# Feed-forward of a four-layer image network: three PSUM banks in turn for the centred tiles, and the slots written out

## What is computed

```
t = t + ffn(layernorm(t))          # 24 -> 96 -> relu -> 24, products in an 8-bit float, sums rounded to fp16
x = x + next_mixer(layernorm(x))   # the mixer of the following layer begins with a norm over the channels
```

## Time and profile before

| | us |
|---|---|
| median of three runs (lowest, highest) | 3311.95 (3308.96, 3316.39) |
| the profiled execution's own time | 3312.04 |
| its span, from first to last instruction | 3310.4 |
| busy over the span: PE, DVE, ACT, POOL | 2831.6, 2666.6, 2258.8, 1860.7 |
| stretch 1, from first to last instruction | 462.6 to 629.3 |
| stretch 2 | 1971.3 to 2142.2 |
| stretch 3 | 2676.0 to 2847.2 |
| stretch 4 | 3165.3 to 3307.1 |

### The profile page before, as it was taken

How to read it: one execution, slowest core, us unless ns; L and a number is a source line. 1 busy time by engine, 2 the same in 40 slices (tenths; PEclk the granted TensorE clock), 3 DMA queues, 4 the chain that set the end, 5 groups by cost and what they waited for, 6 DMA issues and landing times. The chain is left out here.

```text
span 3310.4 us, 65685 instructions
## 1 busy us (share of the span) xinstructions
PE 2831.6 (86%) x20846; PEld 1477.4 (45%) x20846; DVE 2666.6 (81%) x4380; ACT 2258.8 (68%) x4205; POOL 1860.7 (56%) x1466
## 2 busy tenths in 40 slices
PE   8999989686999999999997678789999779688876
PEld 5666654233444444444442224344444334477732
DVE  6888879536999999999999958769999968444468
ACT  5666658576999898989895427666777558444455
POOL 2333323155889898989897635447777745100046
PEclk9999999898999999999999999989999989899999
DMA  2000001256474747474746232201101012301023
GB/s 88 0 0 0 0 14 45 81 172 175 120 209 135 221 140 222 140 217 141 217 124 185 59 79 74 76 21 25 24 23 25 18 56 89 126 22 23 22 71 78
DMA packets 201533, 294.28 MB, mean 89 GB/s; under 512 B 62242, under 2 KB 179158, under 8 KB 201110
## 3 DMA queue, kind: packets, MB, share of 16 engines
q1 hardware_dynamic: 198678, 288.03, 30.3%
q10 hardware_dynamic: 2688, 4.29, 0.4%
HBM read 190.11 MB, written 102.09 MB: 88 GB/s over the span
## 5 line engine op out<-in xcount | busy, mean ns | idle before, releaser
L1780 POOL TENSOR_TENSOR mam_hc<-mam_h,mam_cs 128x896 f32<-128x896 f32 x336 | 703.5, 2094 | 173.5 <-DVE mam_h L1699 98.7
L1699 DVE TENSOR_TENSOR_SCAN mam_h<-mam_a,mam_kept,mam_dbx 128x448 f32<-128x448 f32 x672 | 737.7, 1127 | 48.4 <-ACT mam_a L1569 47.4
L1422 PE MATMUL mam_ps_y<-mam_hc,mam_ident 128*128 128x448 f32 x1344 | 570.8, 558 | 124.8 <-POOL mam_hc L1780 124.7
L1569 ACT ACTIVATE mam_a<-mam_ft,mam_a_neg 128x448 f32<-128x448 f32 x672 | 409.5, 657 | 77.1 <-DVE mam_h L1699 76.0
L1422 PEld LDWEIGHTS mam_ps_y<-mam_hc,mam_ident 128*128 128x128 f32 x1344 | 249.8, 193 | 425.4 <-POOL mam_hc L1780 216.2
L1686 DVE TENSOR_TENSOR mam_dbx<-mam_ps_u,mam_bs 128x448 f32<-128x448 f32 x672 | 380.7, 610 | 0.0
L682 POOL TENSOR_TENSOR att_prob<-att_prob,att_share 128x588 f32<-128x588 f32 x128 | 149.0, 1186 | 306.8 <-DVE att_share L974 306.8
L2209 POOL TENSOR_TENSOR scan_ch<-scan_h,scan_cs 128x392 f32<-128x392 f32 x192 | 263.7, 1387 | 56.5 <-DVE scan_h L2150 55.3
L368 POOL MEMSET f_squares_ln<- 128x392 f32 x4 | 1.7, 424 | 362.5 <-POOLq L2283 326.5
L387 POOL CAST f_h<-f_hr 128x392 fp8e5<-128x392 f16 x128 | 65.3, 510 | 234.1 <-DVE f_hr L308 234.1
L2150 DVE TENSOR_TENSOR_SCAN scan_h<-scan_decay_by_column,scan_h,scan_drive_by_column 128x392 f32<-128x392 f32 x112 | 196.8, 1757 | 0.0
(11 more groups left out here) (240 smaller groups left out, 6631.1 us busy)
## 6 DMA issues: line engine op xcount, KB each, us to landing
mam_taps<-normed SPq DMA_DIRECT2D x220, 130.5 KB
mam_bs<-dram_bc SPq DMA_DIRECT2D x56, 448.0 KB, 9.1
mam_cs<-dram_bc SPq DMA_DIRECT2D x56, 448.0 KB, 11.7
normed<-f_staged SPq DMA_DIRECT2D x96, 203.0 KB
mam_ft<-dram_steps SPq DMA_DIRECT2D x42, 448.0 KB, 4.8
f_mixed<-mixed SPq DMA_DIRECT2D x64, 196.0 KB, 2.4
mam_gt<-dram_gs SPq DMA_DIRECT2D x48, 224.0 KB, 2.7
dram_gs<-mam_gs SPq DMA_DIRECT2D x47, 224.0 KB, 2.8
```

The costliest lines, as they stand in the source:

```text
L1422: mm = pe.matmul(ps_y[p % 2][:, 0:MT], ident[:], hc[t % 2][:, i, :], start=False, stop=(t % 8 == 7 and i == 1))
L1569: act.activation(a[t % 3][:, i, :], ft[p % 2][:, 0, :], ACT.Exp, scale=a_neg[:, at:at + 1]).then_inc(decays, 1)
L1699: dve.tensor_tensor_scan(h[:, n % 8, :], a[t % 3][:, i, :], dbx[:, i, 0:MT], kept[:, at:at + 1], ALU.mult, ALU.add).then_inc(scanned, 1)
L1780: pool.tensor_tensor(hc[t % 2][:], h[:, row:row + 2, :], cs[:, 2 * pair:2 * pair + 2, :], ALU.mult).then_inc(weighed, 1)
```

## The change

The two banks of the feed-forward norm and the one of the mixer's norm become a ring of three. Centred tiles are written in one fixed order (norm of chunk s-3, then feed-forward of chunk s+1), and each takes the next bank of the ring. So the mixer's centred tile no longer waits for the tile of its own kind before it; the feed-forward tile that follows now waits for that (`normed` of chunk c-5 is behind `c - 4` in the code). All slots are written out on PE, ACT and DVE, with constant wait values. On POOL the loop is written with another index.

```diff
-        fronts = [buf.psum(f"xc_ff{p}", [P, BANK]) for p in range(2)]
-        xc_ln = buf.psum("xc_ln", [P, BANK])
+        ring = [buf.psum(f"centred{p}", [P, BANK]) for p in range(3)]
...
-            with eng.Fori(0, CHUNKS // UNROLL - 1) as t:
-                for i in range(3, 3 + UNROLL):
-                    slot(t * UNROLL + i, t + i // UNROLL, i % UNROLL, [True] * 4)
...
+        end = CHUNKS + (2 if last else lag)
+
+        def bank(c):
+            return ring[2 * c % 3]
+
+        def second_bank(c):
+            return ring[(2 * c + 1) % 3]
...
-                quantize_third(0)
-                for c in range(CHUNKS):
-                    if c + 1 < CHUNKS:
-                        quantize_third(c + 1)
-                    update(c)
+                for c in range(CHUNKS + 1):
+                    if is_chunk(c):
+                        quantize_third(c)
+                    if is_chunk(c - 1):
+                        update(c - 1)
                     if c + AHEAD_ADDED < CHUNKS and not in_place:
                         add_mixed(c + AHEAD_ADDED)
...
+                def subtract_mean(c):
+
+                    if not in_place:
+                        pe.wait_ge(ff["added"], c + 1 + ab)
+                    reached(pe, ff["quantized"], c - 2 + fb)
+                    if not last:
+                        reached(pe, ln["normed"], c - 4 + nb)
+                    centre_of(ff, bank(c), c)
+
+                def subtract_mean_again(c):
+
+                    pe.wait_ge(ff["updated"], c + 1 + fb)
+                    pe.wait_ge(ff["quantized"], min(c + 3, CHUNKS) + fb)
+                    reached(pe, ln["normed"], c - 2 + nb)
+                    centre_of(ln, second_bank(c), c)
...
-                slots(pe, slot)
+                for s in range(end):
+                    if is_chunk(s - 1):
+                        hidden_units(s - 1)
+                    if is_chunk(s - 2):
+                        second_product(s - 2)
+                    if not last and is_chunk(s - lag):
+                        subtract_mean_again(s - lag)
+                    if is_chunk(s + 1):
+                        subtract_mean(s + 1)
+                    if not last and is_chunk(s - lag):
+
+                        pe.wait_ge(ff["summed16"], min(s - 1, CHUNKS) + fb)
+                        variance(ln, "ln", nb, s - lag)
+                    if is_chunk(s + 1):
+                        variance(ff, "ff", fb, s + 1)
```

More of the change, by code:

```diff
@@ L188, in feed_forward_phase, with is_chunk @@
         lag = 3
[L190 to L195, removed]
-            with eng.Fori(0, CHUNKS // UNROLL - 1) as t:
-                for i in range(3, 3 + UNROLL):
-                    slot(t * UNROLL + i, t + i // UNROLL, i % UNROLL, [True] * 4)
[L199 to L205, removed]
+        end = CHUNKS + (2 if last else lag)
[3 more added lines that the diff above has]
+            return ring[(2 * c + 1) % 3]
+        def is_chunk(c):
+            return 0 <= c < CHUNKS
         def dram_rows(dram, j, g, start, length):
@@ L287, in quantize @@
                     dve.memset(gate[:, 0:1], 0.0)
[L288 removed]
+                    dve.tensor_tensor(xq[:], bank(c)[:, 0:N], rstd["ff"][:], ALU.mult,
                                       saturate=False).then_inc(ff["quantized"], 1)
@@ L426, in round_hidden @@
                                    ).then_inc(ff["hidden16"], 1)
-                def slot(s, turn, u, on):
-                    if on[0]:
+                square(ff, "ff", fb, 0)
+                for s in range(end):
+                    if is_chunk(s):
                         inverse_deviation(ff, "ff", fb, eps_t, "quantized", s)
-                    if on[1]:
+                    if is_chunk(s - 1):
                         round_hidden(s - 1)
[L433 to L436, removed]
-                    if not last and on[3]:
+                    if not last and is_chunk(s - lag):
+                        square(ln, "ln", nb, s - lag)
+                    if is_chunk(s + 1):
+                        square(ff, "ff", fb, s + 1)
+                    if not last and is_chunk(s - lag):
                         inverse_deviation(ln, "ln", nb, eps_c, "normed", s - lag)
-                square(ff, "ff", fb, 0, 0)
-                slots(act, slot)
             @block.tensor
@@ L497, in second_product @@
                     for t in range(THIRDS):
[L498 removed]
+                        mm = pe.matmul(ps_y[:, 0:N], w2[:, t, :], h8[c % 2][:, t, :],
                                        start=(t == 0), stop=(t == THIRDS - 1))
                     mm.then_inc(ff["summed"], 1)
[L502 to L524 removed]
+                subtract_mean(0)
+                variance(ff, "ff", fb, 0)
                 multiply_zeros(2)
                 pe.wait_ge(st.prepared, prep0 + preps)
[L527 removed]
+                for s in range(end):
+                    if is_chunk(s - 1):
+                        hidden_units(s - 1)
+                    if is_chunk(s - 2):
+                        second_product(s - 2)
+                    if not last and is_chunk(s - lag):
+                        subtract_mean_again(s - lag)
+                    if is_chunk(s + 1):
+                        subtract_mean(s + 1)
+                    if not last and is_chunk(s - lag):
+                        pe.wait_ge(ff["summed16"], min(s - 1, CHUNKS) + fb)
+                        variance(ln, "ln", nb, s - lag)
+                    if is_chunk(s + 1):
+                        variance(ff, "ff", fb, s + 1)
+                    if s < 2:
+                        multiply_zeros(2)
 LAYERS = 4
```

77 lines of the change are left out of this document (21 added, 56 removed).

## The result

The changed kernel takes 3321.48 us (median of 12 runs, 3309.65 to 3328.5), the kernel before, measured beside it, 3311.84 us (12 runs, 3307.55 to 3316.58): a ratio of 1.0026, 95% interval 1.0016 to 1.0037, so 5 to 12 us slower. The forecast was 3323 us. The profiled execution took 3324.02 us, 11.98 us more than that of before.

What follows compares the result with a forecast made beforehand. Chains through the single bank (4.54 us a slot) and through f_y (4.51) bound the kernel; early adds would close a longer one. Terms -5.2 + 10.8 + 10.5 - 4.5 = +11.6 us gave 3323 us, range 3317 to 3332.

Steps and rivals of the forecast that it cites:

- POOL's adds, stretches 2 and 3: Early adds wait for loads behind stores, closing a 10.32 us chain over two slots: +13.9 and +13.6 us before tails.
- Stretch 1, slots: Stretch 1: chain through xc_ln goes, chain through f_y stays at 4.51 us a slot: -2.1 us over 27 slots.
- Code loading: Loop bodies fetched as straight code on the engines: costed at nothing, at most 3 us.
- Tails: Last chunks of stretches 1 to 3: centred tile no longer waits for the single bank, -3.1 us each, ends 2.6 and 4.
- Stretch 4: Stretch 4: early add leaves PE's path, 3.78 us a slot against 3.94: -4.5 us, ends -2 and -8.
- Sum: All four stretches: -5.2 + 10.8 + 10.5 - 4.5 = +11.6 us against 3312.04, predicted 3323 us.
- A: Rival for POOL's adds: they find their data, no stall; -22.2 us, 3290 us; chance 0.12.
- B: Rival: stall stays, but faster landing, stretch 4 at -8 and tails of 4 us outweigh more; 3315 us; chance 0.22.
- C: Rival for stretches 2 and 3: every slot, not every second, pays the long time; 34 us more, 3357 us; chance 0.06.

Runs made afterwards that it cites:

- short rounding: Changed kernel with AHEAD = 7 in place of 6, in which DVE's f_y takes only 8 of its 392 columns: 3262.98 us, ratio 0.9842.
- short CAST: Changed kernel with AHEAD = 7 in place of 6, in which DVE's CAST h8 takes 8 of 392 columns of each third: 3278.6 us, ratio 0.9889.
- straight code alone: All slots written out with constant waits, but the kernel before's banks with their waits and POOL's old order: 3302.44 us, ratio 0.9968.
- late adds: Changed kernel with POOL's old loop, each add one step later; ring and written-out slots stay: 3286.31 us, ratio 0.9922.
- loads seven ahead: Changed kernel with AHEAD = 7 in place of 6, POOL's early adds kept: 3282.05 us, ratio 0.9908; repeated, 3281.98 us, ratio 0.9914.
- loads five ahead: Changed kernel with AHEAD = 5 in place of 6, each load issued one chunk later: 3746.38 us, ratio 1.1318.
- short add: Changed kernel in which POOL's add takes 8 of its 392 columns, behind the same wait: 3294.29 us, ratio 0.995.

## Why the prediction was right, point by point

**POOL's adds, stretches 2 and 3.** Forecast +13.9 and +13.6 us for the slots; measured +14.2 and +11.1. The chain and its closing over two slots are shown by five runs: without POOL's new order it is gone, with the order alone it is there, with one load earlier it is gone, with one load later it closes in each slot, and with 0.8 us less work in it the period falls by as much. Its size was a little too large. From add to centred tile I added up whole durations, 1.03 + 0.51 + 0.93 + 0.16 = 2.63 us; POOL's rows overlap by 0.07 and 0.04 us and PE follows sooner, so it took 2.41. The slot shown has a load of 2.76 us from issue to add that makes up for it; half of the links were 10.1 us or shorter, so stretch 3 is the typical one (13 x 10.1 + 4.5 = 136). Stretch 2 reached my number by luck, through one pair of slots of 12.7 us (`staged` at 2012.06 and 2024.73): its add came 5.4 us behind `staged`, 1.5 later than usual, and behind this pause PE ran at a granted clock of 0.50 (2019.4 to 2022.7 us), which took another 1.2:

```profile
2019.84 2.98 PE L441 MATMUL f_centred<-all_x,f_centre 128*128 128x392 f32 x4
```

The same four rows take 1.58 us at 2051.20.

**Stretch 1, slots.** Forecast 4.51 us a slot, -2.1 us; measured 121.9 against 123.9, with the variance waiting 32.2 us for `f_y`. The short rounding and the short CAST show that this chain sets the period. The share that I gave to the bank (0.02 or 0.03 us a slot) was wrong: it is nothing. So was "the single bank is thus a limit of the period": the slot of 4.54 us that I read it from was one of the short ones of a loop whose slots take 4.62 us on average, and in straight code the same bank allows 4.51.

**Code loading.** Forecast nothing, at most 3 us. The run with straight code alone bears this out: its slots are at 4.51 us, as above.

**Tails.** Forecast -3.1 us each. In stretches 2 and 3 they went from 18.5 and 19.2 to 15.1 us: -3.4 and -4.1, at the upper end that I had named. In stretch 2 the last centred tile stands right behind the update. In stretch 1 it does not. The timeline of the two tails:

```profile
622.14 0.93 POOL L368 TENSOR_TENSOR all_x<-all_x,f_yb 128x392 f32<-128x392 f32 x1 [2.71 <-DVE f_yb L322]
...
623.09 1.64 PE L464 MATMUL f_ps_y<-f_squares_ln,f_average 128*128 128x392 f32 x2 [0.68 <-ACT f_squares_ln L396]
...
624.53 1.51 PE L441 MATMUL f_centred<-all_x,f_centre 128*128 128x392 f32 x2
...
2140.76 0.92 POOL L368 TENSOR_TENSOR all_x<-all_x,f_yb 128x392 f32<-128x392 f32 x1 [2.22 <-DVE f_yb L322]
...
2141.79 0.87 PE L441 MATMUL f_centred<-all_x,f_centre 128*128 128x392 f32 x2
```

and the windows of 620 to 625 us, with the granted clock behind the busy times:

```profile
620.00:625.00 5.00, 4.32 (x9) 2.05 (x10) 1.46 (x3) 0.85 (x3) 0.93 (x1) 0.50 0.11 42
```

In stretch 1 the update ends at 623.07, but PE is at its variance, which takes 1.64 us where it takes 0.90 otherwise, and writes the tile at 624.53. PE's granted clock is 0.50 here, the lower of the two levels (1.2 GHz). The tail of stretch 1 fell by 1.0 us only. This is what I had allowed half a microsecond for. The same tail took 15.1 us in the run with late adds, so here it belongs to the execution, not to POOL's order. But it is no rare case: of the 27 tails in the nine traces with the ring 22 took 14.8 to 15.1 us, and five, in which the granted clock fell to 0.61 to 0.80, took 17.3 to 19.5 us; the longest, stretch 1 with loads seven ahead (clock 0.61), is as long as with the old banks, where all nine tails took 18.3 to 20.0. At the entry of stretch 1 (455 to 475 us) the clock was 0.74 on average, where before had 1.00, and the first `xq` came 3.1 us later behind the stretch's first instruction. This distance is 7.6 us in the three traces with the old banks and 7.6, 9.3 or 10.2 to 10.7 in the nine with the ring, whose clock there lies between 1.00 and 0.74; why, stays open. Stretch 1 as a whole: -0.3 us for -5.2.

**Stretch 4.** Forecast -4.5 us, ends -2 and -8; measured +1.0 (28 slots +0.8). This step failed: neither the gain nor the path was right. The tile views of the third `h_r` in stretch 4 (ns: least, median, largest), before and after:

```profile
L308 DVE TENSOR_SCALAR f_hr<-f_h,f_b x32: 308/313/322, 3179.9 to 3301.1; 128x392 f16<-128x392 f16 x32
...
L300 DVE TENSOR_SCALAR f_hr<-f_h,f_b x32: 304/486/1025, 3191.0 to 3313.0; 128x392 f16<-128x392 f16 x32
```

the waits of 3200 to 3310 us:

```profile
PEld f_ps_y L488 <- DVE f_h L310: 25.1, 28, 1.6
POOL all_x L362 <- DMA f_mixed<-mixed: 22.6, 24, 2.0
```

and rows of the timeline:

```profile
3250.20 1.01 POOL L362 TENSOR_TENSOR all_x<-all_x,f_mixed 128x392 f32<-128x392 f32 x1 [1.01 <-DMA f_mixed<-mixed]
...
3250.50 0.83 DVE L300 TENSOR_SCALAR f_hr<-f_h,f_b 128x392 f16<-128x392 f16 x1
...
3251.26 0.55 DVE L316 CAST f_y<-f_ps_y 128x392 f16<-128x392 f32 x1
3251.40 0.51 POOL L375 CAST f_h<-f_hr 128x392 fp8e5<-128x392 f16 x1 [0.18 <-DVE f_hr L300]
...
3252.35 0.94 POOL L368 TENSOR_TENSOR all_x<-all_x,f_yb 128x392 f32<-128x392 f32 x1 [0.44 <-DVE f_yb L322]
```

The add waits about 1 us for its load in most slots, 22.6 us in all, starts late, and falls on DVE's third `h_r`, which takes 0.83 us here in place of 0.31; the 32 of the stretch sum to 17.3 us, where they took 10.0. POOL's CAST waits for that `h_r`, and what DVE does behind it is late too: `f_y`, the bias `f_yb`, for which POOL's update waits 0.44 us, and `h8`, for which PE waits 25.1 us (17.8 us with loads seven ahead). With the load earlier the add is in time, `h_r` takes 0.31 us again, and the stretch gives -6.9 us (103.5 us), inside the range that I had given. With late adds it gives -0.8 us. So the store, the load and the add are in the chain as I had it, but behind the add it doesn't close through POOL's CAST and update, which both wait for DVE here; it closes through DVE's `h_r`, `f_y` and `f_yb`, and two slots take 7.9 us (from the end of the update at 3245.38 to that at 3253.29). The way through POOL, which I had summed to 7.50, measures 7.21 us in the run with loads five ahead; over two slots that is 3.6 us a slot, less than the 3.69 that stretch 4 takes when the data are in time, so it would have bound nothing. How much of the loss is the add's lateness and how much what it does to `h_r` the runs don't separate, since the short add is over in 0.20 us and takes away both. That POOL waits is not the cost here either: with the short add it still waits 30.1 us for the loads of stretch 4 (3165 to 3275 us), and the slots take 104.0 us.

**Sum.** -0.3 + 10.4 + 6.6 + 1.0 = +17.8 us in the stretches (the forecast: +11.6), and the rest of the profiled execution was 5.8 us shorter, 6.4 of it in the mixers between stretches 1 and 2 (1342.0 to 1335.6 us). The change doesn't touch their code. Over the traces of this study that part took 1339 to 1342 us in three traces with the old banks and 1330 to 1341 us in nine with the ring; whether the ring has a hand in it stays open. That the total came so near to the forecast is in part luck: the misses of stretches 1 and 4 (+10 us) were made up by stretch 3 (-4) and the mixers (-6).

**Rivals.** A (no stall) is refuted by the wait of 74.7 us; its 3290 us are near what the change gives once the adds find their data (3286 with late adds, 3282 with early loads). B named gains of which two came, the tails of stretches 2 and 3 (3.4 and 4.1) and a chain of 10.1 us (not by a faster landing, though, but by the 2.41 us above); stretch 4 did not join them. C (each slot pays) is refuted: pairs of slots, 10.27 us. It would have been right with one load later.

## What to carry to other kernels

A wait that POOL, or any engine, can afford is set by what stands behind it in program order. Before an operation is moved one step ahead, ask when its data arrive, and what the arrival itself waits for: here the load stood behind a store that waited for the end of the same slots, and one step turned slack into a closed loop. The price of such a loop is its length divided by the number of slots that it spans, less the slot that the other chains ask, and not the time shown as waiting; moving the load by one step (one constant) took away 39 us. A moved operation can also meet another engine's in time, as in stretch 4: read which operation it now falls on. And a visible wait for a buffer is no reason for more buffers until a run without that wait shows another period.

## What the runs showed of the hardware

POOL and DVE hold each other up. DVE's CAST of `h8` (784 columns) takes 0.56 us while POOL rests (first row, with loads five ahead) and 1.17 us when it begins under POOL's update (second row, before; the update runs from 3232.41 to 3233.34):

```profile
3623.33 0.56 DVE L310 CAST f_h<-f_hr 128x784 fp8e5<-128x784 f16 x1
...
3232.60 1.17 DVE L318 CAST f_h<-f_hr 128x784 fp8e5<-128x784 f16 x1
```

Cut to 16 columns it still takes 0.77 us, as these rows of the timeline show, in which it starts during POOL's update (2042.08 to 2043.01) and ends 0.03 us after it:

```profile
2042.08 0.93 POOL L370 TENSOR_TENSOR all_x<-all_x,f_yb 128x392 f32<-128x392 f32 x1 [0.44 <-DVE f_yb L324]
2042.27 0.77 DVE L312 CAST f_h<-f_hr 128x16 fp8e5<-128x16 f16 x1
```

The time thus doesn't go with the columns of DVE's operation, it goes with the end of POOL's. The third `h_r` of stretch 4 is the same: it ends 0.12 us after the add. The other way round POOL's add takes 1.33 us in place of 1.02 when it starts during `h8` (3233.30, while the CAST above ends at 3233.77). Operations that read PSUM (`f_y`, `xq`, 0.55 to 0.57 us) do not change under either: 0.55 to 0.57 us in every row of `f_y` of the kernel before and of the changed one. The Trainium skill (SBUF — State Buffer, "Who interferes with whom") states this as an exclusive lock on a port pair that the two engines share, taken for the whole instruction, and not by DVE operations with a single SBUF input outside its faster modes; the durations above agree in order and in direction, though not to the tenth of a microsecond: behind the update's end the whole CAST needs 0.43 us more, where alone it takes 0.56, and the add is 0.31 us longer for an overlap of 0.47. What I had not weighed is that moving an operation of POOL in time chooses which of DVE's operations is held up.
